# A later start of the expert blocks, another order of the front slots, and a new form of the normalisation, in a four-layer attention and expert kernel

## The chip, the cores and the metric

One core of one Trainium2 chip runs the whole program in one launch. The metric is the device time in microseconds, from one launch to its end. The five engines have a program each and meet through semaphores: TensorE (PE; its weight loads are PEld), VectorE (DVE), ScalarE (ACT), GpSimd (POOL) and SyncE (SP, which only issues DMAs).

## The reference, cut to what matters

The input x is 32 sequences of 64 rows of 128 numbers, float32, so 2048 rows; a context of the same shape is attended to. Each layer adds an attention and then a second part, both of the normalised x:

```
x = x + L0_xattn(layernorm(x), ctx)      # 16 heads of 64
x = x + L0_ffn(layernorm(x))             # six layers of local attention and a gated FFN
x = x + L1_xattn(layernorm(x), ctx)      # 16 heads of 8                      (n = 0)
x = x + L1_ffn(layernorm(x))             # rows quantised to fp8, one 128x128 product
x = x + L2_xattn(layernorm(x), ctx)      # 16 heads of 8                      (n = 1)
x = x + L2_moe(layernorm(x))             # shared expert and 8 routed, top 2   (e = 0)
x = x + L3_xattn(layernorm(x), ctx)      # 16 heads of 8                      (n = 2)
x = x + L3_moe(layernorm(x))             # 8 experts, top 2, cosine gates      (e = 1)

# an attention: softmax(q k^T / sqrt(8)) v per head (n = 1 without the root), then @ Wo + bo
# L1_ffn: s = max|row| / 448; fp8(row / s) * s @ (w * ws).T + bias
# a moe:  sum over experts of gate[:, e] * (gelu(x @ Wfc[e] + b) @ Wproj[e] + b2), 128 -> 512 -> 128
```

## The kernel before, in words

x stays in on-chip memory as 16 tiles of 128 rows (two sequences each); four tiles are a quad (q = 0 to 3). The first attention and the six FFN layers come first, up to 1729 us of the profile. All that follows, from `n = 0` to the end, is the merged stage, and the change is in it alone but for the normalisation, which the first attention uses too.

The merged stage is a static schedule of 85 slots, numbered u. Each engine's program walks through the slots in the same order, and what it does in a slot is written out in a fixed order. An engine waits at an instruction whose semaphore isn't there yet, and all that follows on that engine waits with it. Two kinds of work go through the slots:

- **A work** is one tile through one of the three attentions (48 works). It takes three slots: in slot u PE turns the normalised tile (`turn_x`), computes keys, values and queries; in u+1 the scores, on which DVE runs `shift` (largest per head, L1765, and its subtraction, L1767), ACT the exponential (L1682), and PE turns the probabilities (`turn_probs`, L1536); in u+2 PE attends (L1481), DVE divides (`scale_rows`, L1774 and L1777), PE turns the rows (`turn_rows`, L1504) and multiplies by the output weights (`rows`, L1530), and DVE adds them to x (L1790). Then x is normalised again for the next part: statistics on DVE (L598, L600), the root on POOL (L611, L613), the result on DVE (L605, into `y_all`: "fresh"). The tile that starts in slot u+1 is normalised in slot u in the same way (L605 into `normed`).
- **A job** is one expert for one quad (68 jobs, from slot `LEAD` = 15 on, one in each slot): PE computes four hidden chunks of 128 (L1402), ACT their gelu (L1652), POOL multiplies them by the gate, two chunks at a time (L1927, not for the ungated expert 8), and one slot later PE multiplies by the second weights (L1413) into one bank. Jobs of one layer and quad are a block, of 9 jobs for e = 0 and 8 for e = 1; `block(e, q)` is its first slot. Around a block come `TURN` (the normalised quad turned), `RAW` (e = 1), `LOGITS`, `GATES` (DVE ranks the logits and makes the gates, L1823 to L1847, and ACT has an exponential in between), then PE turns the gates (L1455) in the same slot, ACT copies them (L1750), SP stores them to memory and spreads them, one DMA for each job, over 128 partitions.

Slots 0 to 14, without jobs, are the front slots. In them PE issues an idle matmul twice (`occupy`, L1544: the result isn't used), once behind the queries and once behind `rows`. The fp8 part of a quad is in two slots: in `QUANTISE_AT` (6, 10, 22, 26) DVE quantises (L1864 to L1873) behind the fresh normalisation, and PE turns the result as the last thing of the slot (L1572); in the next, `PRODUCT_AT`, PE starts with the product (L1580), ACT with its copy (L1706), DVE with its addition to x (L1879).

Results that go through PSUM share three banks (`ring_uses`, `claim`): a use waits until the use before it in its bank has been read. On DVE a front slot runs: statistics and normalisation of the next tile, `shift`, `scale_rows`, keys (L1783), `add_rows`, fresh statistics, fresh normalisation, quantising. With jobs, `scale_rows` comes ahead of `shift`. On POOL a slot runs: bias, root of the next tile, first gated multiply, fresh root, second gated multiply.

## Time and profile before

| what | us |
|---|---|
| median of 3 runs | 2611.71 (2608.36 to 2612.85) |
| the profiled execution, its own time | 2607.74 |
| its span, first to last instruction | 2606.0 |
| PE busy | 2411.4 (93%) |
| DVE busy | 1916.2 (74%) |
| ACT busy | 1468.5 (56%) |
| POOL busy | 1477.3 (57%) |

The shares are means over the whole program. They say that PE is the fullest engine; where PE waits, and for what, has to be read from its gaps. PE stands at 93% of the span but in the first slots of the merged stage at only three quarters, and there its granted clock is below full speed too. A busy time of PE contains slow matmuls: the same four turns can stand in the trace with one duration or with nearly twice it, by the clock that was granted.

### The profile page before, as it was taken

The numbers are of one execution on the slowest core, as the hardware profiler recorded it, in microseconds if no ns is written. First come the engines' busy times: TensorE is split into PE (matmuls) and PEld (weight loads), VectorE is DVE, ScalarE is ACT, GpSimd is POOL, SyncE is SP. The second block draws the span as 40 slices with busy tenths as digits, with TensorE's granted clock in tenths as the row PEclk, the third lists the DMA queues.
The fourth block names the chain that finished last, engine by engine and source line by source line (L and its number), as shares of the span: only waits on it lengthen the run. The fifth ranks groups of instructions, "written<-read, shape, count | busy, mean of one in ns | idle before, by whom it ended". The sixth has DMA issues, their size and how long they took to land.

```text
span 2606.0 us, 61086 instructions
## 1 busy us (share of the span) xinstructions
PE 2411.4 (93%) x25544; PEld 1449.5 (56%) x25544; DVE 1916.2 (74%) x3344; ACT 1468.5 (56%) x2059; POOL 1477.3 (57%) x995
## 2 busy tenths in 40 slices
PE   6887899999999999999999999877798899999999
PEld 5775566566566565665666666634444444454444
DVE  4666899989999999999999999656677677444110
ACT  2332656666666666666666666533366666566443
POOL 1222776766777777767667777411143445555655
PEclk9998999999999999999999999988899999999999
DMA  3000000100000000001000000001010101120111
GB/s 119 5 5 5 2 2 2 34 2 12 21 15 7 7 26 10 12 2 34 2 13 26 10 7 5 2 25 61 6 39 6 38 6 39 44 76 20 37 37 40
DMA packets 35752, 55.95 MB, mean 21 GB/s; under 512 B 6094, under 2 KB 20456, under 8 KB 35244
## 3 DMA queue, kind: packets, MB, share of 16 engines
q1 hardware_dynamic: 35500, 52.33, 6.5%
q8 instruction: 190, 3.11, 0.5%
q14 instruction: 62, 0.51, 0.1%
HBM read 51.13 MB, written 1.19 MB: 20 GB/s over the span
## 4 chain that ended last, share of the span: by engine, by line
PE 47%; DVE 27%; issue 11%; ACT 11%; POOL 4%; SPq 0%; DMA 0%; DVEq 0%; POOLq 0%; ACTq 0%
PE w L1402 7%; PE w L1413 7%; DVE turned L1056 4%; DVE norm L1063 4%; PE w L765 4%; PE w L790 4%; PE w L778 4%; PE py L803 4%; PE w L519 3%; DVE straight_odd L1051 2%; DVE top L568 2%; PE w L856 2%; DVE y_all L605 2%; ACT sq L1002 2%; ACT sq L993 2%
## 5 line engine op out<-in xcount | busy, mean ns | idle before, releaser
L593 POOL TENSOR_TENSOR prob<-prob,rden 128x1024 f32<-128x1024 f32 x112 | 213.3, 1905 | 206.4 <-DVE rden L582 206.4
L563 ACT ACTIVATE prob<-logit 128x512 f32<-128x512 f32 x224 | 137.6, 630 | 281.1 <-DVE logit L571 281.1
L1172 POOL TENSOR_TENSOR straight_odd<-straight_odd,turned 128x1024 f32<-128x1024 f32 x96 | 227.3, 2369 | 82.9 <-DVE turned L1056 80.0
L1402 PE MATMUL w<-qT,m_fc 128*128 128x512 f32 x544 | 274.3, 618 | 0.0
L1172 POOL TENSOR_TENSOR straight<-straight,turned 128x1024 f32<-128x1024 f32 x96 | 226.7, 2370 | 44.1 <-DVE turned L1056 44.1
L1166 POOL TENSOR_TENSOR straight_odd<-straight_odd,rnorms 128x1024 f32<-128x1024 f32 x96 | 180.6, 1902 | 116.7 <-DVE rnorms L1077 116.7
L1056 DVE TENSOR_TENSOR turned<-w,rot 128x512 f32<-128x512 f32 x384 | 245.5, 681 | 0.0
L1063 DVE TENSOR_REDUCE norm<-sq 128x16 f32<-128x1024 f32 x192 | 224.2, 1209 | 0.0
L1166 POOL TENSOR_TENSOR straight<-straight,rnorms 128x1024 f32<-128x1024 f32 x96 | 180.5, 1901 | 72.4 <-DVE rnorms L1077 72.4
L1927 POOL TENSOR_TENSOR turned<-turned,b_wqkv 128x1024 f32<-128x1024 f32 x64 | 149.8, 2351 | 80.3 <-DMA b_wqkv<-gates 40.2
L765 PE MATMUL w<-b_wqkv,m_proj 128*128 128x512 f32 x384 | 192.3, 623 | 2.9 <-DVE turned L1056 1.6
L790 PE MATMUL w<-b_wqkv,m_proj 128*128 128x512 f32 x384 | 190.8, 619 | 0.0
L1010 ACT COPY qT<-w 128x1024 f32<-128x1024 f32 x96 | 97.3, 1014 | 157.9 <-PE w L815 157.9
L778 PE MATMUL w<-b_wqkv,m_proj 128*64 128x512 f32 x768 | 186.0, 605 | 0.0
L611 POOL TENSOR_TENSOR fresh_roots<-fresh_means,eps 128x1 f32<-128x1 f32 x64 | 12.3, 191 | 293.9 <-DVE fresh_means L600 293.8
L803 PE MATMUL py<-oT,b_wo 128*128 128x256 f32 x768 | 175.7, 382 | 1.1 <-ACT oT L1031 1.1
L1927 POOL TENSOR_TENSOR straight_odd<-straight_odd,b_wqkv 128x1024 f32<-128x1024 f32 x64 | 150.5, 2363 | 44.5 <-ACT straight_odd L1652 35.2
L803 PEld LDWEIGHTS py<-oT,b_wo 128*128 128x128 f32 x768 | 147.1, 192 | 42.0 <-issue 22.8
L1002 ACT ACTIVATE sq<-w 128x1024 f32<-128x1024 f32 x96 | 98.2, 1023 | 115.0 <-PE w L790 115.0
L519 PE MATMUL w<-probT,v 64*64 64x64 f32 x7168 | 131.7, 223 | 24.7 <-ACT probT L1015 19.6
L1652 ACT ACTIVATE turned<-w,m_bfc 128x512 f32<-128x512 f32 x136 | 93.4, 688 | 106.7 <-PE w L1402 104.4
L1652 ACT ACTIVATE straight_odd<-w,m_bfc 128x512 f32<-128x512 f32 x136 | 93.3, 687 | 105.0 <-PE w L1402 101.9
(260 smaller groups left out, 5548.2 us busy)
## 6 DMA issues: line engine op xcount, KB each, us to landing
b_wqkv<-gates SPq DMA_DIRECT2D x64, 256.0 KB, 4.1
b_wqkv<-in_b_wqkv SPq DMA_DIRECT2D x18, 512.0 KB, 3.6
ctxT<-in_ctxT SPq DMA_DIRECT2D x64, 64.0 KB, 1.8
b_wo<-in_b_wo SPq DMA_DIRECT2D x6, 512.0 KB, 3.8
m_fc<-in_m_fc SPq DMA_DIRECT2D x1, 2304.0 KB
m_proj<-in_m_proj SPq DMA_DIRECT2D x1, 2304.0 KB
m_fc<-in_m_fc SPq DMA_DIRECT2D x8, 256.0 KB, 3.0
m_proj<-in_m_proj SPq DMA_DIRECT2D x8, 256.0 KB, 3.4
```

Source lines behind the costliest of these rows:

```text
L519: mm = pe.matmul(w[64 * c:64 * c + 64, at:at + 64], k.v2[r, s, b, 64 * h:64 * h + 64], k.probT[r, h, 64 * b:64 * b + 64], start=True, stop ...
L593: pool.tensor_tensor(flat, flat, k.rden[:, s, :, None].broadcast_to([P, HEADS, SEQ]), ALU.mult).then_inc(k.prob_ready, 1)
L765: mm = pe.matmul(k.w0[:, 512 * c:512 * c + 512], shifted_rows(k, g % TILES), k.b_wqkv[:, 512 * c:512 * c + 512], start=True, stop=True)
L778: mm = pe.matmul(k.w2[64 * p:64 * p + 64, 512 * b:512 * b + 512], k.z[:, 2 * t + b, :], k.b_wqkv[:, 2048 + 512 * p:2560 + 512 * p], start= ...
L790: mm = pe.matmul(k.w1[:, 512 * c:512 * c + 512], shifted_rows(k, g % TILES), k.b_wqkv[:, 1024 + 512 * c:1536 + 512 * c], start=True, stop= ...
L803: mm = pe.matmul(k.py[:, 0:2 * P], k.b_wo[:, h, :], k.oT[:, h, :, :].rearrange("p a n -> p (a n)"), start=(h == 0), stop=(h == PAIRS - 1))
L1056: last = dve.tensor_tensor(k.turned[:, i, :, to], heads[:, :, of], rot[:, 2 * i + 1, None, to].broadcast_to([P, HEADS, half]), ALU.mult)
L1063: dve.tensor_reduce(k.norm2[:, i, :], k.sq[:, i, :, :], AX.X, ALU.add).then_inc(norm2, 1)
L1166: pool.tensor_tensor(k.straights[s][:, i, :, :], k.straights[s][:, i, :, :], k.rnorms[:, s, i, :, None].broadcast_to([P, HEADS, HD]), ALU. ...
L1172: pool.tensor_tensor(k.straights[s][:, i, :, :], k.straights[s][:, i, :, :], k.turned[:, i, :, :], ALU.add).then_inc(added, 1)
L1402: pe.matmul(claim(("hidden", J, c)), k.m_fc[:, x, c * P:(c + 1) * P], k.m_xT[:, q, :], start=True, stop=True).then_inc(k.ring_full, 1)
L1927: pool.tensor_tensor(rows, rows, k.m_gateB[:, g % SPREAD, None, :].broadcast_to([P, 2, 512]), ALU.mult).then_inc(k.h_scaled, 1)
```

## The change

- `normalise_vector` (L605) becomes a `scalar_tensor_tensor`: the mean is still a scalar for each partition, the root becomes a second tensor input, one column broadcast to 128.
- `LEAD` is 16: one more front slot, the jobs start one slot later, and there are 86 slots. The works of quad (0, 2) start at 8, 17, 18, 19; the others are moved by one; slot 24 starts no work.
- Front slots: both idle matmuls stand behind the queries, ahead of `turn_rows`; none is behind `rows`. DVE runs `shift` ahead of the next tile's normalisation (its statistics stay in front).
- fp8: DVE quantises in the same slot as before, PE turns the result in the next slot (behind the second hidden chunk, or in a front slot behind the queries), the product stands at the end of that slot, and DVE adds it one slot later.
- Gates: but for the first block, `TURN`, `RAW`, `LOGITS` and `GATES` are one slot earlier for e = 1 against the block's start; for e = 0 `TURN` is two slots and the others one slot earlier. PE turns the gates one slot after DVE made them, behind the queries. So they are turned in slot `block` for e = 0 (in its middle, not at its end) and `block - 1` for e = 1. For the first block alone the gates are made in slot 16 and turned in slot 17; before, both were in slot 15.
- SP stores and spreads the gates in the slot in which they are turned.

```diff
@@ -602,7 +602,8 @@
     dve.wait_ge(n.rstd, T + 1)
-    return dve.tensor_scalar(to, rows, n.means[:, s, 0:1], n.roots[:, s, :], ALU.subtract, ALU.mult)
+    return dve.scalar_tensor_tensor(out=to, in0=rows, scalar=n.means[:, s, 0:1], in1=n.roots[:, s, :].broadcast_to([P, P]),
+                                    op0=ALU.subtract, op1=ALU.mult)
@@ -1270,7 +1271,7 @@
-LEAD = 15
+LEAD = 16
 NE = (9, 8)
@@ -1278,12 +1279,13 @@
-QUAD_START = {(0, 0): 0, (0, 1): 4, (1, 0): 8, (1, 1): 12, (0, 2): 16, (0, 3): 20, (1, 2): 24, (1, 3): 28,
-              (2, 0): 32, (2, 1): 36, (2, 2): 45, (2, 3): 54}
-WORKS = sorted((first + j, n, 4 * q + j) for (n, q), first in QUAD_START.items() for j in range(4))
+WORK_SLOTS = {(0, 0): (0, 1, 2, 3), (0, 1): (4, 5, 6, 7), (0, 2): (8, 17, 18, 19), (0, 3): (20, 21, 22, 23),
+              (1, 0): (9, 10, 11, 12), (1, 1): (13, 14, 15, 16), (1, 2): (25, 26, 27, 28), (1, 3): (29, 30, 31, 32),
+              (2, 0): (33, 34, 35, 36), (2, 1): (37, 38, 39, 40), (2, 2): (46, 47, 48, 49), (2, 3): (55, 56, 57, 58)}
+WORKS = sorted((slot, n, 4 * q + j) for (n, q), slots in WORK_SLOTS.items() for j, slot in enumerate(slots))
 WORK_AT = {u: (n, t, W) for W, (u, n, t) in enumerate(WORKS)}
 NUMBER = {(n, t): W for n, t, W in WORK_AT.values()}
-QUANTISE_AT = {QUAD_START[0, q] + 6: q for q in range(QUADS)}
+QUANTISE_AT = {WORK_SLOTS[0, q][3] + 3: q for q in range(QUADS)}
 PRODUCT_AT = {u + 1: q for u, q in QUANTISE_AT.items()}
@@ -1312,34 +1314,37 @@
 BLOCKS = [(e, q) for e in range(2) for q in range(QUADS)]
-TURN_AT = {block(e, q) - (3 if e else 1): (e, q) for e, q in BLOCKS}
-RAW_AT = {block(1, q) - 3: q for q in range(QUADS)}
-LOGITS_AT = {block(e, q) - (2 if e else 1): (e, q) for e, q in BLOCKS}
-GATES_AT = {block(e, q) - e: (e, q) for e, q in BLOCKS}
+FIRST_BLOCK = (0, 0)
+TURN_AT = {block(e, q) - (1 if (e, q) == FIRST_BLOCK else 3 + e): (e, q) for e, q in BLOCKS}
+RAW_AT = {block(1, q) - 4: q for q in range(QUADS)}
+LOGITS_AT = {block(e, q) - (1 if (e, q) == FIRST_BLOCK else 2 + e): (e, q) for e, q in BLOCKS}
+GATES_AT = {block(e, q) - (0 if (e, q) == FIRST_BLOCK else 1 + e): (e, q) for e, q in BLOCKS}
+GATES_TURN_AT = {u + 1: block_of for u, block_of in GATES_AT.items()}
 TAIL_AT = {block(e, q) + NE[e] + 1: (e, q) for e, q in BLOCKS}
-SIM_AT = 42
+SIM_AT = 45
...
     for u in range(SLOTS):
+        job = [("hidden", job_at(u)[4], c) for c in range(4)] if job_at(u) else []
+        uses += [(u, use) for use in job[0:2]]
+        if u in PRODUCT_AT:
+            uses.append((u, ("quantised", PRODUCT_AT[u])))
+        uses += [(u, use) for use in job[2:4]]
+        if u in GATES_TURN_AT:
+            uses.append((u, ("gates",) + GATES_TURN_AT[u]))
+        if u in TURN_AT:
+            uses.append((u, ("turn",) + TURN_AT[u]))
         if u in PRODUCT_AT:
             uses.append((u, ("product", PRODUCT_AT[u])))
-        if job_at(u):
-            uses += [(u, ("hidden", job_at(u)[4], c)) for c in range(4)]
-        if u in TURN_AT:
-            uses.append((u, ("turn",) + TURN_AT[u]))
         if u in RAW_AT:
...
             uses.append((u, ("logits",) + LOGITS_AT[u]))
-        if u in GATES_AT:
-            uses.append((u, ("gates",) + GATES_AT[u]))
         if u == SIM_AT:
             uses.append((u, ("sim", 1, 0)))
-        if u in QUANTISE_AT:
-            uses.append((u, ("quantised", QUANTISE_AT[u])))
     where, latest, turn = {}, {}, 0
@@ -1556,6 +1561,9 @@
             queries(work[0], work[2])
+        if u in PRODUCT_AT:
+            turn_quantised(PRODUCT_AT[u])
+        occupy()
         occupy()
@@ -1563,7 +1571,6 @@
             rows(before2[0], before2[2], u)
-        occupy()
@@ -1583,8 +1590,6 @@
         job, last = job_at(u), job_at(u - 1)
-        if u in PRODUCT_AT:
-            product(PRODUCT_AT[u])
         if u < LEAD:
@@ -1596,6 +1601,8 @@
                 hidden(job, 1)
+            if u in PRODUCT_AT:
+                turn_quantised(PRODUCT_AT[u])
             if u in TAIL_AT:
@@ -1613,6 +1620,8 @@
                 queries(work[0], work[2])
+            if u in GATES_TURN_AT:
+                gates(*GATES_TURN_AT[u])
             if u in TURN_AT:
@@ -1625,16 +1634,14 @@
                 turn_probs(before[2])
+        if u in PRODUCT_AT:
+            product(PRODUCT_AT[u])
         if u in RAW_AT:
...
             logits(*LOGITS_AT[u])
-        if u in GATES_AT:
-            gates(*GATES_AT[u])
         if u == SIM_AT:
             sim()
-        if u in QUANTISE_AT:
-            turn_quantised(QUANTISE_AT[u])
@@ -1687,6 +1694,10 @@
+    def turned_quantised(q):
+        turned = full(("quantised", q))[:, 0:256].bitcast(BF16)
+        act.copy(k.f_qT[:, :, :], turned).then_inc(k.ring_read, 1)
+
     def quad_exp(e, q):
@@ -1700,10 +1711,6 @@
         job = job_at(u)
-        if u in PRODUCT_AT:
-            q = PRODUCT_AT[u]
-            act.wait_ge(k.f.done, q)
-            act.copy(k.f_prod, full(("product", q))).then_inc(k.ring_read, 1)
         if u in TAIL_AT:
@@ -1712,6 +1719,9 @@
             gelu(job, 1)
+        if u in PRODUCT_AT and u >= LEAD:
+            turned_quantised(PRODUCT_AT[u])
+        if job:
             gelu(job, 2)
@@ -1720,12 +1730,17 @@
         if u < LEAD:
+            if u in PRODUCT_AT:
+                turned_quantised(PRODUCT_AT[u])
             if before:
...
                 turned_probs(before[2])
+        if u in GATES_TURN_AT:
+            e, q = GATES_TURN_AT[u]
+            act.copy(k.m_gateT[0:NE[e], 512 * q:512 * q + 512], full(("gates", e, q))[0:NE[e], :]).then_inc(k.ring_read, 1)
         if u in TURN_AT:
@@ -1737,6 +1752,10 @@
             turned_probs(before[2])
+        if u in PRODUCT_AT:
+            q = PRODUCT_AT[u]
+            act.wait_ge(k.f.done, q)
+            act.copy(k.f_prod, full(("product", q))).then_inc(k.ring_read, 1)
         if u in RAW_AT:
@@ -1745,14 +1764,8 @@
             act.copy(k.m_raw[:, 0:n], full(("logits", e, q))[:, 0:n]).then_inc(k.ring_read, 1)
-        if u in GATES_AT:
-            e, q = GATES_AT[u]
-            act.copy(k.m_gateT[0:NE[e], 512 * q:512 * q + 512], full(("gates", e, q))[0:NE[e], :]).then_inc(k.ring_read, 1)
         if u == SIM_AT:
             act.copy(k.m_simT[:, :], full(("sim", 1, 0))[:, 0:8]).then_inc(k.ring_read, 1)
-        if u in QUANTISE_AT:
-            turned = full(("quantised", QUANTISE_AT[u]))[:, 0:256].bitcast(BF16)
-            act.copy(k.f_qT[:, :, :], turned).then_inc(k.ring_read, 1)
@@ -1885,15 +1898,18 @@
         work, before, before2, after = work_at(u), work_at(u - 1), work_at(u - 2), work_at(u + 1)
-        if u in PRODUCT_AT:
-            add_product(PRODUCT_AT[u])
+        if u - 1 in PRODUCT_AT:
+            add_product(PRODUCT_AT[u - 1])
         if after:
             stats(*after)
+        if after and u >= LEAD:
             normalise(after[1], after[2])
...
             shift(before[2])
+        if after and u < LEAD:
+            normalise(after[1], after[2])
         if before2 and u < LEAD:
@@ -1985,6 +2001,7 @@
+    spread_at = {block_of: u for u, block_of in GATES_TURN_AT.items()}
     gated = [job_at(u)[4] for u in range(SLOTS) if job_at(u) and job_at(u)[2] < 8]
@@ -1995,8 +2012,8 @@
             load_experts(sp, k, a)
-        if u in GATES_AT:
-            e, q = GATES_AT[u]
+        if u in GATES_TURN_AT:
+            e, q = GATES_TURN_AT[u]
             j = e * QUADS + q
@@ -2004,7 +2021,7 @@
             free = LEAD + gated[g - SPREAD] + 1 if g >= SPREAD else 0
-            if u == max(block(e, q) - e, free):
+            if u == max(spread_at[e, q], free):
                 spread(J)
```

## Rows read from the trace of the kernel before

**Rows 1.** One stretch: length, busy PE, PEld, DVE, ACT, POOL; PEclk, DMA, GB/s.
```profile
1729.00:1886.00 157.00, 117.38 (x961) 70.23 (x962) 96.27 (x197) 54.56 (x108) 27.61 (x72) 0.84 0.11 38
```

**Rows 2.** Groups, 1886 to 2606 us: busy us, mean ns, idle before, releaser.
```profile
L605 DVE TENSOR_SCALAR y_all<-x_all,fresh_means,fresh_roots 128x128 f32<-128x128 f32 x35 | 77.2, 2205 | 29.0 <-POOL fresh_roots L613 29.0
...
L1504 PE MATMUL pt<-ident,s_rows 128*128 128x128 f32 x35 | 10.4, 298 | 16.4 <-DVE s_rows L1777 16.4
...
L1455 PE MATMUL w<-ident,m_gate 128*9 128x128 f32 (+1 forms) x32 | 5.2, 290 | 7.3 <-DVE m_gate L1847 7.2
```

**Rows 3.** Timeline of one front slot: start, us, engine, line, [idle before].
```profile
1806.35 1.09 PE L1536 MATMUL w<-ident,prob 128*128 128x128 f32 x8 [0.27 <-ACT prob L1682]
...
1810.32 0.18 DVE L600 BATCH_NORM_AGGREGATE norm_means<-norm_stats 128x2 f32<-128x6 f32 x1
...
1811.66 1.02 PE L1544 MATMUL w<-s_w,ident 128*128 128x512 f32 x2
...
1811.77 1.22 DVE L1765 TENSOR_REDUCE top<-w 128x16 f32<-128x1024 f32 x1
...
1813.02 1.22 DVE L1767 TENSOR_TENSOR logit<-w,top 128x1024 f32<-128x1024 f32 x1
...
1814.27 1.06 ACT L1682 ACTIVATE prob<-logit 128x1024 f32<-128x1024 f32 x1 [1.60 <-DVE logit L1767]
...
1814.78 0.33 PE L1504 MATMUL w<-ident,s_rows 128*128 128x128 f32 x1 [2.09 <-DVE s_rows L1777]
...
1815.38 1.97 PE L1536 MATMUL w<-ident,prob 128*128 128x128 f32 x8 [0.27 <-ACT prob L1682]
```

**Rows 4.** Timeline of a steady slot with an expert.
```profile
1936.81 1.02 PE L1402 MATMUL w<-qT,m_fc 128*128 128x512 f32 x2
...
1939.98 2.35 POOL L1927 TENSOR_TENSOR turned<-turned,b_wqkv 128x1024 f32<-128x1024 f32 x1
...
1940.12 2.29 DVE L605 TENSOR_SCALAR normed<-x_all,norm_means,norm_roots 128x128 f32<-128x128 f32 x1 [1.00 <-POOL norm_roots L613]
...
1942.95 0.33 PE L1504 MATMUL pt<-ident,s_rows 128*128 128x128 f32 x1 [1.03 <-DVE s_rows L1777]
...
1944.69 0.49 PE L1525 MATMUL pt<-xT,s_w 128*128 128x128 f32 x2
...
1949.55 1.02 PE L1402 MATMUL w<-qT,m_fc 128*128 128x512 f32 x2
```

**Rows 5.** Timeline: one VectorE form beside a GpSimd multiply, and alone.
```profile
2323.35 2.35 POOL L1927 TENSOR_TENSOR straight_odd<-straight_odd,b_wqkv 128x1024 f32<-128x1024 f32 x1 [1.02 <-ACT straight_odd L1652]
...
2324.07 1.67 DVE L1823 TENSOR_TENSOR m_logit<-m_raw 128x32 f32<-128x32 f32 x1
...
2464.94 0.19 DVE L1823 TENSOR_TENSOR m_logit<-m_raw 128x32 f32<-128x32 f32 x1 [43.51 <-ACT straight_odd L1652]
```

**Rows 6.** Timeline of a quantising slot in the second stretch.
```profile
1989.47 0.67 DVE L1864 TENSOR_REDUCE f_scale<-y_all 128x4 f32<-128x512 f32 x1
...
1993.72 0.61 PE L1572 MATMUL w<-ident,xnT 128*128 128x128 bf16 x4 [5.81 <-DVE xnT L1871]
...
1994.18 0.22 DVE L1873 TENSOR_SCALAR f_scale<-f_scale,f_ws 128x4 f32<-128x4 f32 x1
...
1995.43 2.02 PE L1402 MATMUL w<-qT,m_fc 128*128 128x512 f32 x2
...
1996.41 1.14 DVE L1879 SCALAR_TENSOR_TENSOR x_all<-xs,f_scale,x_all 128x128 f32<-128x128 f32 x4 [2.01 <-ACT xs L1706]
```

**Rows 7.** Timeline: first block's gates, a late block, a quiet slot.
```profile
1899.36 0.57 ACT L1750 COPY v<-w 9x512 f32<-9x512 f32 x1
...
1904.69 2.36 POOL L1927 TENSOR_TENSOR straight_odd<-straight_odd,b_wqkv 128x1024 f32<-128x1024 f32 x1 [4.39 <-DMA b_wqkv<-gates]
...
2473.45 5.30 PE L1402 MATMUL w<-qT,m_fc 128*128 128x512 f32 x8
...
2589.66 3.60 PE L1402 MATMUL w<-qT,m_fc 128*128 128x512 f32 x8
```

## The prediction

> **What bounds the kernel now.** I read the page first, then PE's gaps by their releaser, then slots of each kind on the timeline, instruction by instruction. Up to 1729 us nothing is touched but the form of the normalisation. The stage behind it has two regimes.
>
> In the front slots (1729 to 1886 us) no engine is full: 157 us for 15 slots, PE busy 117, DVE 96, clock 0.84 [rows 1]. That is a chain. In [rows 3] the reader is to follow it once round: probabilities turned 1806.35, `rows` behind them, next statistics aggregated 1810.32, `shift` 1811.77 and 1813.02, exponential 1814.27, probabilities turned 1815.38. Between 1810.32 and 1811.77 DVE only waits for POOL's root and normalises the next tile. The turning takes 1.97 us at the end of the slot and 1.09 a slot earlier [rows 3]: it falls on the clock's lower level (1.2 of 2.4 GHz) after PE's wait of 2.09 us.
>
> From 1886 us on PE is the bound, with gaps: 16.4 us before `turn_rows`, all for `s_rows`, 7.3 before the gates [rows 2], and 5.81 before a quantised quad is turned [rows 6]. In a steady slot (12.74 us from one job's first matmul to the next's) the normalisation of 0.35 us takes 2.29, since a gated multiply on POOL began 0.14 us ahead of it; it ends 0.07 us after POOL, and PE waits 1.03 [rows 4]. The fresh one does the same (mean 2205 ns [rows 2]).
>
> **1. The normalisation.** Alone, the new form costs what the old does: four of L1879, the same form and size, take 1.14 us [rows 6] against 0.35 for one [rows 3]. The question is whether it still waits for POOL. No row has this form with both inputs in SBUF beside a large POOL instruction. The nearest is a `tensor_tensor` with two SBUF inputs, the second one column for each tile, broadcast: 1.67 us where POOL's multiply is running, ending 0.04 after it, and 0.19 alone [rows 5]. There are five such meetings in the trace, and all five wait. The new form has two SBUF inputs as well, x and the broadcast root. Bounds: it is free (-1.03 us in each of 16 slots, -16.5) or it waits as before and ends a little later, as it then has all its columns to read at one per cycle: I take 0.07 us twice a slot, +2.2. By the nearest row I take +2.2.
>
> The Trainium skill speaks against this change: its page "SBUF — State Buffer", section "Who interferes with whom", says that a DVE instruction with two SBUF inputs contends with a GpSimd instruction that reads SBUF, and that only one with at most one SBUF input outside the two-port modes doesn't. By that the gain is nothing, by the change's name it would be the 16.5; the five meetings agree with the page.
>
> **2. The front slots.** With `shift` first, the chain runs from the aggregation straight into it (0.1 us later): 1806.35 to 1810.32 is 3.97, then 0.10, then 1.25 for the reduction, 1.26 for the subtraction, 1.11 for the exponential: 7.7 us. POOL has no large instruction here, so the form of the normalisation costs nothing. Is PE ready? From the turned probabilities to the first idle matmul it needs 5.31 us [rows 3], of which the idle matmul behind `rows` goes (about 0.9): 4.4, and two idle matmuls (1.02 each at most) make 6.4; `turn_rows` is wanted 0.3 before the next turning, at 7.4. So PE waits about a microsecond, no idle matmul lies in the chain, and with a gap half as long I expect the full clock; the 3.97 above is at full clock. If the clock still falls, 0.9 us for the turning and 0.2 for `rows` come on top.
>
> 16 slots now: three that fill, without `rows` or without its chain, an estimate of 6 each, make 18. Thirteen at 7.7 make 100. Quantising (4.9 us of DVE from 1989.47 to 1994.40 [rows 6]) sits between the fresh normalisation and the next `shift`, so it is in the chain twice: 9.8. `add_product`, 1.2 twice: 2.4. Behind each quantising PE idles about 6 us and then turns slowly: 2.2. The last front slot adds the quad's turn, its copy and the logits, an estimate of 2.6. Sum 135 against 157: **-22**, though there is a slot more. The PE wait for the quantised quad, which closed slots 6 and 10, is not gained whole: DVE's own work is what remains.
>
> **3. One work moved to the front.** The slot it leaves shrinks from 12.74 to that of a job alone, two runs of 3.4 us [rows 7], 6.9: **-5.9**.
>
> **4. fp8 in slots 22/23 and 26/27.** Gone: 5.8 and 0.7 twice, and 2 us twice for the first matmuls after them, at 2.02 in place of 1.02 [rows 6]: -17. New: DVE quantises behind a fresh normalisation that POOL still holds. PE's slot ended at 1987.9 (1993.72 less 5.81), and the quantised quad comes 5.8 later; PE now has two hidden chunks and a turn to do meanwhile, 2.0: 3.8 twice. In slot 27 the next tile's normalisation meets POOL's multiply once more (2.4), `add_product` delays it in slots 24 and 28 (1.2 twice), and about 3 us of slow clock return. Sum **-2**. If the normalisation is free, the quad comes 2.0 earlier, the waits are 1.8 and slot 27 has no second: -11.
>
> **5. Gates on PE one slot later.** All 7.3 us of gaps [rows 2] go, since the gates are ready long before PE turns them. After two of these gaps the next eight matmuls take 5.30 us in place of 3.60 [rows 7]: 3.4 more. What is late next: nothing that PE needs, for in those blocks POOL gets its spread gates earlier than now. **-10.7**.
>
> **6. The first block's gates.** They are the exception: its first gated job is in slot 17, and they are now turned in slot 17, behind the queries: those start 7.9 us into a slot with 1.0 of gap [rows 4], so about 7.2. ACT, with its copies of queries and values ahead and slow matmuls at the slot's start, has the gates copied at 9.3. From the end of that copy to POOL's start pass 4.76 us (1899.93 to 1904.69 [rows 7]): the DMA to memory, its wait, the spread; that is 14.0, and the slot lasts 12.7. So POOL stands at `scale_hidden` until about 1.4 us into slot 18, and behind it on POOL is the fresh root, on which DVE's fresh normalisation and all that follows wait: POOL multiplies to 3.7, root 4.5, multiplies again (DVE's fresh normalisation held) to 6.9, bias and next root 8.4, third multiply with the normalisation held to 10.9, `s_rows` 11.4. PE wants it at 5.1 (1942.95 less 1936.81 less the gap [rows 4]); 1.0 of this wait is there today. **+5.3**, and 1.7 for the slow clock behind such a gap: +7. The rest of the first slots with jobs (gates out of slot 16, into 17): -0.5.
>
> Sum: -22 + 2.2 - 5.9 - 2 - 10.7 + 7 - 0.5 = -32. The profiled execution took 2607.7; 2576. The median of the runs lies 4 us over that execution, so I name 2578.
>
> **The rivals.**
> - *The normalisation is free*, because the broadcast column is read once and then needs no port. For it: L605 today is another form, and no row has the new one beside POOL; against it: the five meetings, whose second input is broadcast too. Then +2.2 becomes -16.5, part 3 is -4.8, part 4 -11, part 6 +5: -60, 2548.
> - *The front clock stays low.* 1.1 us for each of 13 slots: +14, 2592. For it: 0.84 in the stretch [rows 1] and the 1.97 [rows 3]; against it: that came behind a wait of 2.09, and mine is half as long.
> - *Slower.* Two idle matmuls stand ahead of `turn_rows` on PE in every front slot. At full clock PE's load is 6.8 us in a slot of 7.7. Should the clock stand at its lower level for whole slots, it is 13.6 and PE is the chain: 13 x 5.9 = +77 against my sum, 2655. It decides once the mean clock in the front is below 6.8/7.7 = 0.88. Today's 0.84 speaks for it; against it, there PE is busy 75% of the stretch and is slow only behind its waits, and I expect 85% busy.
> - *The fp8 and gate moves give nothing* (another wait takes their place): 2590.
>
> **The numbers.** Forecast 0.68, free normalisation 0.14, low clock in the front 0.10, slower 0.03, moves without effect 0.05. The likeliest has a range of its own of 2562 to 2590; with the free normalisation's upper part and most of the low clock, 2544 to 2592. A measurement of this kernel can tell 0.2% (5 us) from no change: faster 0.96, same 0.01, slower 0.03.
>
> **What would show it.** Right: L605 in the slots with jobs still at 2.2 to 2.4 us, ending about 0.14 after POOL's multiply; front slots with 7.7 us from one `turn_probs` to the next, at 1.09 each; jobs' steady slots at 12.8 to 12.9 with a gap of 1.1 to 1.2 before `turn_rows`; no gap before L1455; one gap of 5 to 6 us before `turn_rows` in slot 18, with POOL released by the DMA of the gates; gaps of about 3.8 before L1572 in slots 23 and 27. Wrong: L605 at 0.35 everywhere and steady slots of 11.5 to 11.7 (then 2548); `turn_probs` at 1.97 in the front; a front chain that passes through something other than DVE.

## The result and the profile after

| | before | after |
|---|---|---|
| median, us | 2612.28 (2608.36 to 2614.43) | 2580.87 (2577.86 to 2583.22) |
| the profiled execution, its own time | 2607.74 | 2579.42 |
| its span | 2606.0 | 2577.6 |

The ratio is 0.9881, 95% interval [0.9864, 0.9898]: 31 us faster. The prediction said 2578, with 2544 to 2592 around it. Lines have moved: L1407 are the jobs' hidden chunks, L1499 the scores, L1509 `turn_rows`, L1541 `turn_probs`, L1549 the idle matmuls, L1460 the gates' turn, L1579 the quantised turn, L1778 and L1780 `shift`, L1689 the exponential, L1943 the gated multiply; L605 is still the normalisation.

First the engines' line of the page, which hardly differs from before (PE was 2411.4, also 93%). It doesn't show where the time went.

```profile
PE 2400.9 (93%) x25548; PEld 1445.1 (56%) x25548; DVE 1924.3 (75%) x3344; ACT 1462.7 (57%) x2056; POOL 1476.7 (57%) x995
```

Next the front as one stretch, with the columns of [rows 1]. It is the same work and one slot more, in 135 us for 157; the clock is 0.93 for 0.84.

```profile
1731.40:1866.60 135.20, 111.34 (x1030) 66.79 (x1031) 100.83 (x206) 56.68 (x115) 29.15 (x77) 0.93 0.12 45
```

Once round the chain of a front slot, to be held against [rows 3]. From the aggregated statistics (1813.70) to `shift` it is 0.10 us, where it was 1.45; the next tile is normalised behind `shift`, while ACT starts the exponential. PE fills its time with four idle pieces (two idle matmuls) and waits 1.04 before `turn_rows`. The turning takes 1.09 in every round. From one turning to the next are 7.81 us.

```profile
1809.59 1.09 PE L1541 MATMUL w<-ident,prob 128*128 128x128 f32 x8
...
1813.70 0.18 DVE L600 BATCH_NORM_AGGREGATE norm_means<-norm_stats 128x2 f32<-128x6 f32 x1
1813.80 1.19 DVE L1778 TENSOR_REDUCE top<-w 128x16 f32<-128x1024 f32 x1
...
1814.14 1.88 PE L1549 MATMUL w<-s_w,ident 128*128 128x512 f32 x4
...
1815.03 1.23 DVE L1780 TENSOR_TENSOR logit<-w,top 128x1024 f32<-128x1024 f32 x1
1816.17 0.34 DVE L605 SCALAR_TENSOR_TENSOR normed<-x_all,norm_means,norm_roots 128x128 f32<-128x128 f32 x1
1816.29 1.06 ACT L1689 ACTIVATE prob<-logit 128x1024 f32<-128x1024 f32 x1 [1.14 <-DVE logit L1780]
...
1817.06 0.33 PE L1509 MATMUL w<-ident,s_rows 128*128 128x128 f32 x1 [1.04 <-DVE s_rows L1790]
1817.40 1.09 PE L1541 MATMUL w<-ident,prob 128*128 128x128 f32 x8
```

The groups from 1866 us on answer to [rows 2]. The normalisation in its new form takes 2220 ns in the mean, as long as the old one (2205). The gates' gaps are down from 7.3 to 1.6, the wait for `s_rows` is up from 16.4 to 26.9, and 6.2 stand before the quantised turn.

```profile
L605 DVE SCALAR_TENSOR_TENSOR y_all<-x_all,fresh_means,fresh_roots 128x128 f32<-128x128 f32 x35 | 77.7, 2220 | 32.9 <-POOL fresh_roots L614 32.9
...
L1509 PE MATMUL pt<-ident,s_rows 128*128 128x128 f32 x34 | 10.6, 313 | 26.9 <-DVE s_rows L1790 26.9
...
L1460 PE MATMUL w<-ident,m_gate 128*9 128x128 f32 (+1 forms) x32 | 4.8, 273 | 1.6 <-DVE m_gate L1860 1.6
...
L1579 PE MATMUL w<-ident,xnT 128*128 128x128 bf16 x8 | 1.0, 263 | 6.2 <-DVE xnT L1884 6.2
```

A steady slot (12.87 us, [rows 4] had 12.74). The normalisation starts 0.13 behind the multiply and ends 0.15 after it, and PE waits 1.16.

```profile
1922.98 1.02 PE L1407 MATMUL w<-qT,m_fc 128*128 128x512 f32 x2
...
1926.21 2.34 POOL L1943 TENSOR_TENSOR turned<-turned,b_wqkv 128x1024 f32<-128x1024 f32 x1
1926.34 2.36 DVE L605 SCALAR_TENSOR_TENSOR normed<-x_all,norm_means,norm_roots 128x128 f32<-128x128 f32 x1 [0.99 <-POOL norm_roots L614]
...
1929.25 0.33 PE L1509 MATMUL pt<-ident,s_rows 128*128 128x128 f32 x1 [1.16 <-DVE s_rows L1790]
...
1935.85 1.02 PE L1407 MATMUL w<-qT,m_fc 128*128 128x512 f32 x2
```

Slots 17 and 18, where the first block's gates arrive. ACT has them copied at 1886.69, GpSimd starts 4.70 later (4.76 in [rows 7]), behind 10.53 us of idling, and the fresh normalisation and all behind it come late: 6.18 us of gap, then matmuls at half speed (1.91).

```profile
1886.12 0.57 ACT L1743 COPY v<-w 9x512 f32<-9x512 f32 x1
...
1891.39 2.36 POOL L1943 TENSOR_TENSOR straight_odd<-straight_odd,b_wqkv 128x1024 f32<-128x1024 f32 x1 [10.53 <-DMA b_wqkv<-gates]
...
1894.55 2.42 DVE L605 SCALAR_TENSOR_TENSOR y_all<-x_all,fresh_means,fresh_roots 128x128 f32<-128x128 f32 x1 [5.98 <-POOL fresh_roots L614]
...
1901.35 0.47 PE L1509 MATMUL pt<-ident,s_rows 128*128 128x128 f32 x1 [6.18 <-DVE s_rows L1790]
...
1902.05 1.91 PE L1407 MATMUL w<-qT,m_fc 128*128 128x512 f32 x2
```

Slot 23, the quantising. It meets GpSimd twice: the normalisation ahead of it (2.45) and its own first product (2.82, where it is 0.69 alone). PE waits 6.19.

```profile
1961.44 2.45 DVE L605 SCALAR_TENSOR_TENSOR y_all<-x_all,fresh_means,fresh_roots 128x128 f32<-128x128 f32 x1 [0.92 <-POOL fresh_roots L614]
...
1964.87 2.34 POOL L1943 TENSOR_TENSOR straight_odd<-straight_odd,b_wqkv 128x1024 f32<-128x1024 f32 x1 [0.67 <-ACT straight_odd L1659]
1964.93 2.82 DVE L1880 TENSOR_TENSOR y_all<-y_all,f_rscale 128x512 f32<-128x512 f32 x1
...
1970.18 0.61 PE L1579 MATMUL w<-ident,xnT 128*128 128x128 bf16 x4 [6.19 <-DVE xnT L1884]
```

In slots (from one slot's first matmul to the next one's), the front takes 135.2 us, not 156.8, and all behind it 711.0, not 719.9. Slot 0 starts at 1731.4, not 1729.3. Up to there the two programs differ only in the form of the normalisation. In the profiles below that start lies between 1729.3 and 1735.1, and not by the form: the run with the old form (e1) has it at 1732.3, one with the new form (e6) at 1729.3. That much an execution varies by itself. So parts are compared by their slots, whole kernels by the ratio.

### The profile page after: what moved, and what is told of

The parts are those of the page before. It is cut to its first block, busy times and chain, and to the rows that moved or that the text cites. A ratio compares the mean times of both kernels' runs of the same rounds, so it can differ in the third digit from the quotient of the medians.

```text
span 2577.6 us, 61085 instructions
## 1 busy us (share of the span) xinstructions
PE 2400.9 (93%) x25548; PEld 1445.1 (56%) x25548; DVE 1924.3 (75%) x3344; ACT 1462.7 (57%) x2056; POOL 1476.7 (57%) x995
## 4 chain that ended last, share of the span: by engine, by line
PE 47%; DVE 27%; issue 11%; ACT 10%; POOL 3%; DMA 0%; SPq 0%; DVEq 0%; POOLq 0%; ACTq 0%
PE w L1418 8%; PE w L1407 7%; DVE turned L1057 4%; DVE norm L1064 4%; PE w L766 4%; PE w L791 4%; PE w L779 4%; PE py L804 4%; PE w L519 3%; DVE straight_odd L1052 2%; DVE top L568 2%; DVE y_all L605 2%; PE w L857 2%; ACT sq L1003 2%; ACT sq L994 2%
## 5 line engine op out<-in xcount | busy, mean ns | idle before, releaser
L1407 PE MATMUL w<-qT,m_fc 128*128 128x512 f32 x544 | 269.3, 607 | 0.4 <-ACT turned L1659 0.4
L1943 POOL TENSOR_TENSOR straight_odd<-straight_odd,b_wqkv 128x1024 f32<-128x1024 f32 x64 | 149.7, 2349 | 60.0 <-ACT straight_odd L1659 49.5
L1943 POOL TENSOR_TENSOR turned<-turned,b_wqkv 128x1024 f32<-128x1024 f32 x64 | 150.3, 2359 | 53.5 <-ACT turned L1659 53.5
L519 PEld LDWEIGHTS w<-probT,v 64*64 64x64 f32 x7168 | 117.3, 137 | 62.4 <-ACT probT L1016 36.2
```

Of the source, the lines that this page charges most:

```text
L519: mm = pe.matmul(w[64 * c:64 * c + 64, at:at + 64], k.v2[r, s, b, 64 * h:64 * h + 64], k.probT[r, h, 64 * b:64 * b + 64], start=True, stop ...
L1407: pe.matmul(claim(("hidden", J, c)), k.m_fc[:, x, c * P:(c + 1) * P], k.m_xT[:, q, :], start=True, stop=True).then_inc(k.ring_full, 1)
L1943: pool.tensor_tensor(rows, rows, k.m_gateB[:, g % SPREAD, None, :].broadcast_to([P, 2, 512]), ALU.mult).then_inc(k.h_scaled, 1)
```

## The experiments

The theory: the front was a chain through DVE, and its order paid; the gates' later turn paid; the new form pays nothing, since it waits for GpSimd as the old one does, and that meeting is the largest thing left. The rivals stand with each run. All ratios are to the kernel before.

| run | median, us | ratio, interval | its slots against after |
|---|---|---|---|
| after | 2580.87 | 0.9881 [0.9864, 0.9898] | |
| e1_old_form | 2579.80 | 0.9881 [0.9865, 0.9897] | -0.2 |
| e2_before_new_form | 2615.29 | 1.0017 [1.0007, 1.0026] | (+5.3 against before) |
| e3_pool_waits | 2555.36 | 0.9788 [0.9773, 0.9802] | -24.4 |
| e4_first_gates | 2574.16 | 0.9860 [0.9843, 0.9876] | -5.0 |
| e5_idle_behind | 2589.07 | 0.9908 [0.9893, 0.9923] | +7.6 |
| e6_no_idle | 2598.49 | 0.9970 [0.9951, 0.9989] | +28.7 |
| e7_shift_behind | 2605.83 | 0.9977 [0.9967, 0.9988] | +24.5 |
| e8_fp8_back | 2587.52 | 0.9906 [0.9891, 0.9922] | +8.2 |
| e9_gates_back | 2585.25 | 0.9898 [0.9883, 0.9913] | +4.6 |
| c1_waits_first | 2552.34 | 0.9771 [0.9758, 0.9784] | -27.8 |
| c2_quantise_waits | 2547.97 | 0.9751 [0.9737, 0.9764] | -33.4 |
| c3_lead15 | 2553.45 | 0.9775 [0.9761, 0.9788] | -28.5 |

### The form of the normalisation

```diff
-    return dve.scalar_tensor_tensor(out=to, in0=rows, scalar=n.means[:, s, 0:1], in1=n.roots[:, s, :].broadcast_to([P, P]),
-                                    op0=ALU.subtract, op1=ALU.mult)
+    return dve.tensor_scalar(to, rows, n.means[:, s, 0:1], n.roots[:, s, :], ALU.subtract, ALU.mult)
```

> The kernel after with one thing undone: the normalisation is a tensor_scalar again. Theory (both forms wait for GpSimd's multiply beside them, the new one a little longer): L605 in the slots with jobs stays above 2.1 us, steady slots go from 12.86 back to about 12.73, the gap before turn_rows from 1.15 to about 1.03, and the run is 2 to 3 us faster than after (ratio 0.999). Rival (the new form contends less, and something else keeps the slot at 12.86): steady slots get longer, by up to 1.2 us each, and the run is 5 to 18 us slower than after.

> The kernel before with the new form of the normalisation and nothing else. Theory: 16 steady slots get 0.14 us longer, plus 2 to 3 us in all (about 2614, ratio 1.001). Rival (the form is free of the wait, as the change's name says): the gap of 1.03 us before turn_rows goes in 16 slots, minus 16 us (about 2596, ratio 0.994).

In the first run steady slots fell to 12.72 with a gap of 1.01, as the theory says, and slots 18 to 40 got 2.7 us shorter. The time didn't: slots 16 and 17 took 26.1 us for 23.4. Behind the same wait of 2.10 us in slot 16 the clock is low there and not in after. The first row is that run, the second after, both five microseconds that begin 0.5 before that wait ends (columns of [rows 1]); the clock is 0.50 in the one and 1.00 in the other:

```profile
1877.50:1882.50 5.00, 4.55 (x13) 2.88 (x13) 2.92 (x12) 3.53 (x5) 1.88 (x5) 0.50 0.00 0
```

```profile
1876.70:1881.70 5.00, 4.49 (x53) 2.79 (x53) 3.41 (x14) 4.13 (x6) 1.88 (x5) 1.00 0.00 0
```

In the second run every steady slot went from 12.73 to 12.86, together 1.8 us. The other 3.5 are nearly all in the front, most in slots 13 and 14 (10.21 and 12.46 us for 8.30 and 11.28), not in the form's own time; why is open. By the ratio the whole run is 4.4 us slower, more than the 2 to 3 that I expected. The rival is out: the form by itself costs 2 us in the steady slots and gains nothing.

### GpSimd's multiplies behind the normalisation

```diff
         if gated:
+            if after:
+                pool.wait_ge(k.norm.normed, PHANTOM + after[2] + TILES + 1)
             scale_hidden(job, 0)
...
         if gated:
+            if before2:
+                pool.wait_ge(k.fresh.normed, PHANTOM + before2[2] + TILES + 1)
             scale_hidden(job, 1)
```

> The kernel after, but GpSimd's two gated multiplies of a slot wait until the normalisation that they meet has been written; nothing else is changed. Theory (the meeting of DVE's normalisation with GpSimd's multiply costs PE its gap of 1.15 us in the steady slots): L605 falls to 0.35 us everywhere, the gap before turn_rows goes, steady slots take 11.6 to 11.8, and the run is 14 to 20 us faster than after, about 2563. In slot 23 the normalisations no longer delay the quantising by 2 us twice, so the gap of 6.2 before the quantised turn falls to 2 to 4. Rival (the waits push GpSimd's work later, and its scaled chunks or its roots become what PE waits for): L605 is short, but a gap of about the same size stands before output or turn_rows, and the run is within 4 us of after.

Groups from 1869 us on, and a steady slot:

```profile
L605 DVE SCALAR_TENSOR_TENSOR y_all<-x_all,fresh_means,fresh_roots 128x128 f32<-128x128 f32 x35 | 13.1, 373 | 33.3 <-POOL fresh_roots L614 33.3
...
L1509 PE MATMUL pt<-ident,s_rows 128*128 128x128 f32 x34 | 9.8, 288 | 7.5 <-DVE s_rows L1790 7.5
```

```profile
1948.31 0.35 DVE L605 SCALAR_TENSOR_TENSOR normed<-x_all,norm_means,norm_roots 128x128 f32<-128x128 f32 x1 [3.23 <-POOL norm_roots L614]
...
1948.74 2.35 POOL L1943 TENSOR_TENSOR turned<-turned,b_wqkv 128x1024 f32<-128x1024 f32 x1 [0.54 <-DVE normed L605]
```

GpSimd gives way for half a microsecond, DVE gets two back, and a steady slot takes 11.49 us without a gap. Twelve of them give 16.5 us, slots 24 to 28 another 4.8, slot 18 gives 2.3, slot 23 1.4. The whole is over the 20 that I expected: I had counted the steady slots and little of the others. Slot 23 kept a gap of 5.64, not the 2 to 4 that I expected: there the multiply now met the quantiser instead. No gap came up elsewhere; the rival is out.

### The first block's gates, and all gates

```diff
-GATES_TURN_AT = {u + 1: block_of for u, block_of in GATES_AT.items()}
+GATES_TURN_AT = {u + (block_of != FIRST_BLOCK): block_of for u, block_of in GATES_AT.items()}
```

(with PE's turn and ACT's copy of this block at the slot's end; in the second run `GATES_TURN_AT = dict(GATES_AT)`, the same for all blocks)

> The kernel after, but the first block's gates are turned on PE in slot 16, at its end, as the kernel before did it; all other blocks keep the later place. Theory (of the late gates of this one block GpSimd waits 10.5 us, and that costs slot 18 its gap of 6.2 and the slow clock behind it): slot 18 falls from 20.1 to about 13, slot 16 may grow by 0.5, and the run is 6 to 8 us faster than after. Rival (slot 18's length comes from the fresh works that start there, not from the gates): slot 18 stays above 18 and the time is that of after within 1 us.

> The kernel after, but the gates of every block are turned on PE at the end of the slot in which DVE makes them, as before; all else stays. Theory: the gaps before the gates' turn come back with the slow clock behind two of them (plus 7 to 10 us), and the first block's late gates go (minus 6.7, as measured alone): 1 to 4 us slower than after. Rival (DVE makes the gates early enough in these slots, so that only the first block's place matters): 6 to 7 us faster than after, as in the run with the first block alone.

With the first block's gates alone, slot 18 took 12.85 for 20.06, and slots 16 and 17 together 2.36 more: a gap of 0.51 before the gates, the gates' turn itself, and a clock of 0.89 in slot 17 where after has 1.00. I had allowed 0.5 for this, so the run gained 5.0 in its slots (5.5 by the ratios) and not 6 to 8. With all gates back, slots 16 to 18 are nearly the same, and slots 41 to 75 take 10.2 us more than in after. The row of that second run from 1869 us on:

```profile
L1462 PE MATMUL w<-ident,m_gate 128*9 128x128 f32 (+1 forms) x32 | 5.5, 300 | 9.7 <-DVE m_gate L1866 9.7
```

So the later turn is worth 10 us in the later blocks and costs 5 in the first.

### The front: order, idle matmuls

```diff
-        if after and u >= LEAD:
+        if after:
             normalise(after[1], after[2])
```

(the second place of the call, behind `shift`, is gone)

> The kernel after, but in the front slots DVE normalises the next tile before shift, as before; the idle matmuls, the fp8 steps and the gates stay as they are. Theory (the chain of a front slot runs through DVE from the aggregation into shift): a normal front slot gets longer by the wait for the root and the normalisation, 7.8 to 9.1 or 9.2 us, 13 times, so 16 to 18 us slower than after (about 2598). Rival (PE's load of 6.8 with its idle matmuls sets the slot, and the microsecond of gap is slack): slots grow by 0.4 at most, 5 us or less.

```profile
1761.06 0.18 DVE L600 BATCH_NORM_AGGREGATE norm_means<-norm_stats 128x2 f32<-128x6 f32 x1
...
1762.23 0.35 DVE L605 SCALAR_TENSOR_TENSOR normed<-x_all,norm_means,norm_roots 128x128 f32<-128x128 f32 x1 [0.99 <-POOL norm_roots L614]
...
1762.50 1.22 DVE L1778 TENSOR_REDUCE top<-w 128x16 f32<-128x1024 f32 x1
...
1765.52 0.33 PE L1509 MATMUL w<-ident,s_rows 128*128 128x128 f32 x1 [2.16 <-DVE s_rows L1790]
...
1766.12 1.97 PE L1541 MATMUL w<-ident,prob 128*128 128x128 f32 x8 [0.27 <-ACT prob L1689]
```

The root and the normalisation stand in the chain again (1.44 us from aggregation to `shift`). Three of the slots take 9.1, as expected, but six take 10.0 to 10.2: PE's wait has doubled to 2.16, and the turning behind it takes 1.97. I had counted the first and not the second, so the run is 24.5 us slower in its slots and not 16 to 18.

```diff
         occupy()
-        occupy()
...
             rows(before2[0], before2[2], u)
+        occupy()
```

(in the second run both `occupy()` are left out)

> The kernel after, but one of the two idle matmuls of a front slot stands behind rows again, at the slot's end, as before. Theory (their place matters through the clock: PE comes to turn_rows one idle matmul earlier, waits 1.5 to 2.1 us in place of 1.05, and the clock falls to its lower level behind that): turn_probs at 1.97 in the front, slots of 8.9 to 10.1 us, 13 times, 14 to 28 us slower than after. Rival 1 (the idle matmul itself lengthens the chain, by its 0.43 us at full clock): slots of 8.2, about 5 us slower. Rival 2 (it lies beside the chain and the clock holds): slots of 7.8 and the same time within 1 us.

> The kernel after without the two idle matmuls of each front slot. Theory (they hold the clock: without them PE waits about 2 us ahead of turn_rows, 1.05 and twice 0.43 to 0.5, and the matmuls behind run at the lower level): turn_probs at 1.97, front slots of 8.9 to 10.1, 14 to 28 us slower than after. Rival (the chain through DVE sets the slot and the matmuls in it keep their speed): slots of 7.8, within 2 us of after, as in the run with one of them moved.

With one idle matmul behind `rows` the normal slots still take 7.81 with 1.05 of gap: from one `turn_rows` to the next PE has the same work in either order. What grew are slots 1 and 2 (+3.4, a wait of 2.41 and a slow turning), 7 and 11 (15.0 us for 13.6 and 13.4, +1.5 each), and 16 and 17 by the clock (+1.7). Rival 2 had the normal slots right and not the time; my theory had neither. Without idle matmuls the front takes 158.6 us at a clock of 0.65; the time of an execution spread from 2594 to 2616:

```profile
1729.30:1887.90 158.60, 115.28 (x966) 77.81 (x967) 101.32 (x208) 57.01 (x115) 29.38 (x79) 0.65 0.11 38
```

There PE at half speed is in the chain: slots 3 to 5, at a clock of 0.50, take 10.3 us with almost no wait for `s_rows` (0.12); slot 9, at 0.92, takes 7.84. So in a normal slot the two idle matmuls cost nothing (7.81 us, and PE still waits 1.04) and hold the clock. In slots 7 and 11, where they come at half speed behind the quantised turn, they are slightly in the way: in slot 7 of after they take 3.78 us, and `turn_rows` starts 0.4 after `s_rows` is there.

### The fp8 steps

```diff
-        if u in PRODUCT_AT:
-            turn_quantised(PRODUCT_AT[u])
...
         if u == SIM_AT:
             sim()
+        if u in QUANTISE_AT:
+            turn_quantised(QUANTISE_AT[u])
```

(PE's product and ACT's copy first in `PRODUCT_AT`, DVE's addition in the same slot)

> The kernel after, but the quantised quad is turned at the end of the slot in which DVE quantises it, its product is the first thing of the next slot and its addition comes in that slot, as before; schedule of works, order in the front and gates stay. Theory (PE gains by the later place only what it has to do meanwhile, and the waits shrink rather than go): gaps before the quantised turn of about 5.1 us in slots 6 and 10 in place of 3.3 in 7 and 11, and of 5 to 6 at the end of slots 22 and 26, where after has one of 6.2 and none; in all 8 to 14 us slower than after. Rival (the DVE chain sets those slots whatever PE does): within 2 us of after.

The gaps before the two quantised turns in the front (the first row is this run, the second after, from each front's first to last slot):

```profile
L1576 PE MATMUL w<-ident,xnT 128*128 128x128 bf16 x8 | 1.2, 308 | 13.1 <-DVE xnT L1879 13.1
```

```profile
L1579 PE MATMUL w<-ident,xnT 128*128 128x128 bf16 x8 | 1.2, 307 | 6.5 <-DVE xnT L1884 6.5
```

The front took 9.5 us more: its two gaps are 6.6 each, not the 5.1 that I expected. Behind it the old place is *better*: slots 19 to 28 take 2.7 us less with it. Slot 22 has a gap of 5.87, as expected, but slot 26 one of 0.99 and not 5 to 6. So the whole gain of the fp8 move lies in the front.

### Towards a faster kernel

> The kernel after with two things at once: GpSimd's gated multiplies wait for the normalisations, and the first block's gates are turned in slot 16. Theory (two separate costs): slot 18 takes 11.5 us in place of 17.7, and the run is 6 us faster than with the waits alone, about 2549. Rival (with the waits GpSimd is late in slot 18 anyway): 2553 to 2555.

It came out between: slot 18 took 11.48 (-6.25 against the waits alone), but slots 16 and 17 took the 2.36 more that the early gates cost. Then one wait more:

```diff
         if gated:
             if before2:
                 pool.wait_ge(k.fresh.normed, PHANTOM + before2[2] + TILES + 1)
+            if u in QUANTISE_AT:
+                pool.wait_ge(k.f.quantised, QUANTISE_AT[u] + 1)
             scale_hidden(job, 1)
```

> The run with GpSimd's waits and the first block's early gates, and one wait more: in the two slots with jobs in which DVE quantises, GpSimd's second gated multiply waits for the quantised quad. Theory (two of the quantiser's instructions met a multiply, 1.82 us in place of 0.2 and 2.45 in place of 0.7): both at their short length, the gap before the quantised turn in slot 23 falls from 5.6 to 2.2, 3 to 5 us faster than without that wait, about 2548. Rival (GpSimd's late chunks become what PE waits for in slot 23): the gap moves to output, the same time within 1 us.

The quantiser without that wait:

```profile
1953.68 0.68 DVE L1883 TENSOR_REDUCE f_scale<-y_all 128x4 f32<-128x512 f32 x1
1953.84 2.35 POOL L1949 TENSOR_TENSOR turned<-turned,b_wqkv 128x1024 f32<-128x1024 f32 x1 [0.46 <-DVE y_all L605]
1954.39 1.82 DVE L1884 TENSOR_SCALAR f_scale<-f_scale 128x4 f32<-128x4 f32 x1
...
1956.46 0.69 DVE L1886 TENSOR_TENSOR y_all<-y_all,f_rscale 128x512 f32<-128x512 f32 x1
1956.83 2.52 POOL L1949 TENSOR_TENSOR straight_odd<-straight_odd,b_wqkv 128x1024 f32<-128x1024 f32 x1 [0.23 <-ACT straight_odd L1663]
1957.18 2.45 DVE L1887 TENSOR_SCALAR xs<-y_all 128x512 int32<-128x512 int32 x1
```

and with it:

```profile
1953.63 0.17 DVE L1884 TENSOR_SCALAR f_scale<-f_scale 128x4 f32<-128x4 f32 x1
...
1954.77 0.43 DVE L1887 TENSOR_SCALAR xs<-y_all 128x512 int32<-128x512 int32 x1
...
1957.17 0.40 PE L1581 MATMUL w<-ident,xnT 128*128 128x128 bf16 x4 [1.96 <-DVE xnT L1890]
...
2005.37 2.74 POOL L1949 TENSOR_TENSOR turned<-turned,b_wqkv 128x1024 f32<-128x1024 f32 x1 [6.75 <-DVE xnT L1890]
2005.81 2.33 DVE L1892 TENSOR_SCALAR f_scale<-f_scale,f_ws 128x4 f32<-128x4 f32 x1
```

The gap fell from 5.63 to 1.96, and behind so short a wait the matmuls kept their speed (clock 1.00 there, 0.50 without that wait): slot 23 went from 21.46 to 15.10. Slot 27 paid 1.1 us, with a new gap of 0.86 before `turn_rows`: the multiply is released ahead of the quantiser's last two instructions, and the last one, of four columns, meets it and takes 2.33 us (0.22 without that wait), with the next tile's statistics behind it. The intervals of the two ratios overlap, so that this kernel is faster than the one without the wait rests on its slots (5.6 us less). At 2547.97 us it is the fastest of the study, 1.3% under after and 2.5% under before.

```diff
-LEAD = 16
+LEAD = 15
```

(and the quad of block (0, 2) turned two slots ahead of it)

> The previous kernel, with the jobs starting one slot earlier (15 front slots, as before the change, with the works' slots as they are) and the quad of the third block turned one slot nearer its block. Theory (with GpSimd's waits a work costs 4.6 us in a slot with jobs, 11.5 against 6.9, and 7.8 in a front slot of its own): minus 3.2 for the slot, plus up to 2 for the last quad of the front, turned in the slot that writes its last tile: 1 to 3 us faster, about 2546. Rival (the missing slot returns as waits of the first block for its gates or its turned quad): 3 us slower or more.

The rival won: 5.5 us slower than c2. Its slots 14 to 16 take 43.6 us, c2's slots 14 to 17 take 43.8, so the slot that went saved nothing: PE waits 2.46 for the last tile in slot 14, and slot 15 takes 16.5 at a clock of 0.71. The rest is spread over later slots (from its slot 60 on +3.3 against c2's from 61 on, with a second wait of 1.59 for gates in slot 74). That it comes from works that now meet other blocks' turns is not shown.

## Why the prediction was right, step by step

| step | predicted | measured |
|---|---|---|
| 1 the new form waits too | +2.2 | +1.8 in steady slots (e2) |
| 2 the front | 157 to 135 | 156.8 to 135.2 |
| 4 fp8 in slots with jobs | -2 | +2.7 against the old place in after's schedule (e8, slots 19 to 28) |
| 5 gates later | -10.7 | -9.8 (e9: +10.2 in slots 41 to 75, -0.4 in slots 24 to 28) |
| 6 first block's gates | +7 | +5.0 (e4), 5.5 by the ratios |
| 3 one work moved, and the rest of the slots | -6.4 | about -8.6, what is left of -8.9; no run undid the schedule alone |

**1.** As forecast, and the rival of a free normalisation is out by the rows of both forms: 2220 against 2205 ns. As a whole the form cost the kernel before 4.4 us (e2) and nothing readable in after (e1, the same ratio). The row of another instruction with two SBUF inputs [rows 5] was the right neighbour. The Trainium skill's page "SBUF — State Buffer", section "Who interferes with whom", said that this form contends; the trace agrees (2.36 us beside the multiply, 0.34 in the front).

**2.** The chain was named right: 7.8 us a slot for 7.7, a gap of 1.04 for about 1, full clock in the normal slots (the mean of 0.93 comes from the slow pieces, such as those behind the quantised turns). The two quantisings cost 13.3 us above normal slots (13.59 + 8.76 + 13.39 + 8.76 less four times 7.8) for the 14.4 that I had, the last slot 2.4 for 2.6. The runs split the front in a way that my sum didn't: undoing the order costs 22.5 there, undoing the fp8 place 9.5, one idle matmul 5.6, together more than the 29.4 that was gained (21.6 and a slot of 7.8). They overlap, since each of them alone brings more slow clock with it: 0.89, 0.88 and 0.90 in the front, where after has 0.93.

**4.** The step that failed. I had two gaps of 3.8, in slots 23 and 27. In slot 23 it is 6.2: beside the normalisation, the quantiser's own product waits for GpSimd's next multiply (2.82 us for 0.69), and I had taken the quantiser at its length alone. In slot 27 it is none, since no work starts in slot 24 and so slot 26 has no fresh tile ahead of the quantising. That fault is in my reading of the schedule, not of the trace. It hides in the sum: slots 22 to 28 took 101.1 us for 107.8, -6.7, where steps 3 and 4 together had -7.9. The gap of 5.8 in slot 26 of before, which I gave to the fp8 move, went with the work that slot 24 no longer starts, since with the old place in the new schedule it is 0.99 (e8). So one gap came out longer and the other not at all, the gain of the schedule was larger and that of the move was none, and that the two terms nearly came out together is luck.

**5** and **6.** Mechanism and place right: gates off PE's path but for 1.6 us in slot 67, where the last gate product too meets a multiply; the first block's late by the path that I drew (POOL released 1.33 us into slot 18 for 1.4, gap 6.18 for 6.3). Step 6 was 2 us too dear, because the early gates have a price too: the 2.36 in slots 16 and 17.

**Slower** did not come: the front's clock is 0.93, and e6 shows what lies on that side, 0.65 and PE in the chain. But the bound of 0.88 that I gave for it was wrong. The kernel before stood at 0.84 and still waited 1.4 to 2.1 us for `s_rows` in every normal slot. A mean clock doesn't say where the slow pieces lie; PE comes into the chain where whole slots run at 0.50, as in slots 3 to 5 of e6.

## What to carry to other kernels

When DVE and GpSimd collide, don't look for a cheaper form first; look at which of them can wait. A semaphore that holds GpSimd's long multiply for 0.5 us behind a DVE instruction of 0.35 us was worth 24 us here, the rewritten form nothing. Two thirds of it came in twelve steady slots, where PE had waited 1.15 us for what DVE made behind that instruction. Release the long one only when the short ones behind it are through as well: in the fastest kernel one of four columns still lost 2.1 us. Move a step on PE where its wait can be filled, and look at each place by itself: the same fp8 move gained 9.5 us in the front and lost 2.7 behind it. And in a chain-bound stretch an idle matmul that fits into the gap is no waste; it costs when it is taken away.

## What the runs showed of the hardware

- Which DVE instruction waits for a GpSimd multiply is a matter of form, not of size. A `TENSOR_SCALAR` of four columns took 1.82 us beside one and 0.17 alone; a `TENSOR_REDUCE` of 512 columns from SBUF, begun ahead of the multiply and overlapping it by 0.5 us, kept its 0.68. `shift` and `scale_rows`, which read PSUM, kept their times beside it (1.22 and 0.29 us). Where DVE was first, GpSimd paid: its multiply took 2.52 us beside the end of a two-input product, not 2.35.
- The same wait of PE (2.1 us in slot 16) comes with the full clock level in after and e3 (slot 16: 11.5 us) and with the low one in e1, e5, e7 and e8 (12.3 us), though that slot's work is the same but for e1's form, which differs by 0.07 us a front slot. One execution of each was profiled, so whether this goes with the kernel or with the execution is open. A difference of 2 to 3 us between near equal kernels can be that alone; e1 was faster in every steady slot and the same in sum.
